# A graph layer and a routed feed-forward layer on one core: the affine branch moved to channels on partitions, and four programs joined into one

## The reference

```python
# layer 1
xh = layernorm(x)
theta = gcn_conv(xh, edges, W1, b1)          # (6250, 64), then only its mean over nodes is used
theta = relu(mean(theta, axis=0)) @ W2 + b2  # (1024,)
theta = 2 * sigmoid(theta) - 1
a0, a1, c0, c1 = per channel, from theta     # a0 = 1 + t0, a1 = t1, c0 = t2 / 2, c1 = t3 / 2
x = x + maximum(xh * a0 + c0, xh * a1 + c1)
# layer 2, 16 experts, 2 chosen for each row
xn = layernorm(x)
logits = xn @ gate_w + gate_b;  top 2, softmax over the two
h = relu(xn @ w1[e] + b1[e]);   y = h @ w2[e] + b2[e]
x = x + layernorm(xn + weighted sum of the two y) * gamma + beta
```

## Time and profile before

| | |
|---|---|
| median of 3 runs | 1049.39 us (1049.09 to 1052.37) |
| the profiled execution's own time | 1059.64 us |
| its span | 1057.8 us |
| mean granted TensorE clock | 0.821 |
| busy: PE / DVE / ACT / POOL | 698.1 / 687.2 / 417.3 / 456.7 us |
| DMA | 178.11 MB, mean 168 GB/s |

### The profile page before, as it was taken

One profiled execution on the slowest core, in us unless ns is written; L12 is line 12 of the kernel. 1 busy time (PEld: TensorE's weight loads), 2 busy tenths in 40 slices (PEclk: granted clock), 3 DMA queues, 4 the chain that ended last, 5 costly groups with the idle time before them and its releaser, 6 DMA issues. The chain is left out here.

```text
span 1057.8 us, 21646 instructions
## 1 busy us (share of the span) xinstructions
PE 698.1 (66%) x6132; PEld 609.6 (58%) x6132; DVE 687.2 (65%) x1486; ACT 417.3 (39%) x1089; POOL 456.7 (43%) x655
## 2 busy tenths in 40 slices
PE   3666878887515334230499999999999999970000
PEld 3553655555204333230399999999999999960000
DVE  7998999999269988812145555555444444435984
ACT  5933777776112222220133333333334333321331
POOL 9200000000002888845057777777555555540422
PEclk9997899999655555555599999999999999995555
DMA  9906756752171342224677766767676676625672
GB/s 290 247 7 49 191 160 159 174 173 52 57 237 51 116 143 98 84 74 141 242 210 216 211 212 212 214 211 212 213 214 211 212 211 213 211 81 174 243 240 70
DMA packets 100597, 178.11 MB, mean 168 GB/s; under 512 B 25247, under 2 KB 69153, under 8 KB 97055
## 3 DMA queue, kind: packets, MB, share of 16 engines
q1 hardware_dynamic: 75092, 145.28, 45.8%
q0 software_dynamic: 10512, 27.88, 7.5%
q10 hardware_dynamic: 14880, 3.60, 2.8%
HBM read 139.53 MB, written 37.20 MB: 167 GB/s over the span
## 5 line engine op out<-in xcount | busy, mean ns | idle before, releaser
L1133 PEld LDWEIGHTS PS<-W 128*128 128x128 f32 x1808 | 221.8, 193 | 8.7 <-issue 2.1
L1133 PE MATMUL PS<-W 128*128 128x128 f32 x1808 | 222.6, 277 | 2.2 <-DMA W<-in_L_ffn_w 1.7
L1144 PE MATMUL PS<-W 128*128 x904 | 213.7, 379 | 0.0
L1144 PEld LDWEIGHTS PS<-W 128*128 128x128 f32 x904 | 164.1, 191 | 17.5
L1291 POOL DMA_INDIRECT ys<-W x113 | 121.6, 1076 | 115.5 <-DVE W L1249 88.2
L691 DVE TENSOR_TENSOR W<-R,W 128x3584 bf16<-128x3584 bf16 (+1 forms) x104 | 159.4, 1590 | 0.0
L859 POOL DMA_INDIRECT xs<-W,slot_i x98 | 120.9, 1234 | 88.2 <-DVE slot_i L1008 59.9
L1221 DVE TENSOR_SCALAR W<-PS,b1T 128x128 f32<-128x128 f32 x226 | 70.2, 347 | 115.3 <-PE PS L1133 84.5
L1174 ACT ACTIVATE W<-PS 128x256 f32<-128x256 f32 x113 | 43.3, 383 | 257.3 <-PE PS L1121 155.2
L544 ACT ACTIVATE W<-PS 112x1024 f16<-112x1024 f32 x104 | 105.7, 1020 | 40.1 <-PE PS L603 38.7
L863 POOL MEMSET R<- 128x261 f32 x1 | 0.3, 317 | 254.3 <-POOLq L360 254.3
(11 more groups left out here) (215 smaller groups left out, 1154.5 us busy)
## 6 DMA issues: line engine op xcount, KB each, us to landing
W<-in_L_ffn_w SPq DMA_DIRECT2D x129, 512.0 KB, 8.8
W<-key_rows SPq DMA_DIRECT2D x26, 896.0 KB
W<-xs SPq DMA_DIRECT2D x113, 130.5 KB
W<-ys SPq DMA_DIRECT2D x6, 1792.0 KB, 8.1
XH<-in_x SPq DMA_DIRECT2D x6, 896.0 KB, 11.2
W<-in_x SPq DMA_DIRECT2D x7, 768.0 KB
out<-W SPq DMA_DIRECT2D x6, 896.0 KB, 4.1
W<-in_L_ffn_b ACTq DMA_DIRECT2D x1, 2048.0 KB, 7.5
```

Of the source, the lines that this page charges most:

```text
L1133: last = nc.tensor.matmul(PS[:, 2 + 2 * u + j // 2, (j % 2) * P:(j % 2 + 1) * P], W1S[:, b, k, j * P:(j + 1) * P], XT3[:, u, k, :], start= ...
L1144: last = nc.tensor.matmul(PS[:, 6 + u, 0:C], HT3[:, u, j, :], wt2(e * W2COLS, j), start=(j == 0), stop=(j == 3))
```

## The change

- The coefficients are columns. W2 and b2 are loaded at the start. Eight small products (instead of two of 512 columns) put the 1024 values of theta on 128 partitions x 8, so that each channel has its four coefficients on its own partition. ScalarE's sigmoid table is loaded ahead (`warm`), and the square root's right after the sigmoid.
- The affine branch works with channels on partitions. A group is cut into a chunk of 4 tiles and one of 3. TensorE turns a chunk of XH into PSUM (`turn1`), ScalarE makes both affine forms of it with scale and bias by partition (`affine`: 4 instructions of 512 or of 384 elements), VectorE takes one maximum (`widest`), TensorE turns the result back (`back`), and VectorE adds x to it straight from PSUM (`add_x`). There is one PSUM area for `turn1`, so chunk q+1 is turned after chunk q has been read.
- `xn` has three buffers (XNBUFS). One PSUM bank holds the turned tiles of `turn2`. The prefix of a group stands in TensorE's order after `turn2` of the next, and VectorE's `route` is split in two, `route` and `place`. Loops are written out.
- x for the first two groups is loaded among the last key loads of the first stage, and the other half of the w2 weights before the rest of x.
- Everything is one `nc.Block()`. SP loads four w1 matrices before it waits for the scattered rows. After the last scatter of the experts SP waits for their landing and loads `ys`.
- In the last stage XH is added by VectorE, not by POOL.

```diff
+                def turn1(q):
+                    g, j0, n = CH[q]
+                    if q >= 1:
+                        pe.wait_ge(affined, q)
+                    for j in range(n):
+                        for k in range(2):
+                            last = nc.tensor.transpose(TA[:, j, k, :], XH[:, DG[g][0] + j0 + j, k * P:(k + 1) * P], ident[:, :])
+                    last.then_inc(turned1, 1)
...
-                act.activation(theta, gb2_bc, ACT.Sigmoid).then_inc(sig_ready, 1)
+                act.activation(zcol[:, :, :], zcol[:, :, :], ACT.Sigmoid).then_inc(sig_ready, 1)
+                act.activation(warm[:, 1:2], ones1[:, :], ACT.Sqrt).then_inc(warmed, 1)
+
+                def affine(q):
+                    g, j0, n = CH[q]
+                    act.wait_ge(turned1, q + 1)
+                    if q >= 2:
+                        act.wait_ge(returned, q - 1)
+                    for k in range(2):
+                        for into, s, c in ((bra, 0, 2), (brb, 1, 3)):
+                            last = act.activation(into[q % 2][:, k, 0:n, :], TA[:, 0:n, k, :], ACT.Identity,
+                                                  bias=coef[:, k, c:c + 1], scale=coef[:, k, s:s + 1])
+                    last.then_inc(affined, 1)
...
+                for i in range(-3, NDG - 1):
+                    for q in GCH[i + 3][1:] if i + 3 < NDG else ():
+                        turn1(q)
+                    if 0 <= i + 4 < NDG:
+                        turn1(GCH[i + 4][0])
+                    if i + 3 < NDG:
+                        back(GCH[i + 3][0])
+                    if 0 <= i + 2 < NDG:
+                        turn2(i + 2)
+                    if 0 <= i + 1:
+                        prefix(i + 1)
+                    for q in GCH[i + 3][1:] if i + 3 < NDG else ():
+                        back(q)
+                    if 0 <= i + 2 < NDG:
+                        gate(i + 2)
...
-                    link(nc.vector.tensor_tensor(branch, rows, cb[0], ALU.mult))
-                    link(nc.vector.tensor_tensor(branch, branch, cb[2], ALU.add))
-                    link(nc.vector.tensor_tensor(rows, rows, cb[1], ALU.mult))
-                    link(nc.vector.tensor_tensor(rows, rows, cb[3], ALU.add))
-                    link(nc.vector.tensor_tensor(rows, rows, branch, ALU.max))
...
+                    nc.vector.tensor_tensor(XH[:, t:t + n, :], TB[:, 0:n, :], x_in[:, g % 2, 0:n, :], ALU.add).then_inc(x_added, 1)
...
+                    nc.vector.tensor_tensor(scaled[u], scaled[u], XH[:, g * GT:(g + 1) * GT, :], ALU.add
+                                            ).then_inc(out_ready, 1)
```

More of the change, by code:

```diff
@@ L40 @@
 NGT = NT // GT
+DG = [(k * GT, GT) for k in range(NGT)]
+NDG = len(DG)
+CH, GCH, T2 = [], [], [0]
+for _g, (_t, _n) in enumerate(DG):
+    GCH.append([])
+    for _j in range(0, _n, 4):
+        GCH[-1].append(len(CH))
+        CH.append((_g, _j, min(4, _n - _j)))
+    T2.append(T2[-1] + -(-_n // 2))
 CAP = 6400
@@ L188, in build @@
         home = take([XBUFS], i32)
+        at[0] = D_AT + 4 * XNBUFS * GT * XW
+        b2_bc = take([E, C], fp32)
         gamma_bc = take([C], fp32)
@@ new lines, in build, with x_loads, sends, pad_row @@
+        tab_ready = sem("tab_ready")
+        tab_turned = sem("tab_turned")
+        tables_out = sem("tables_out")
+        def x_loads(g):
+            return 16 * (g // 2 + 1) + (16 if g == NDG - 1 else 0)
+        def sends(g):
+            return 16 * 2 * sum(DG[h][1] for h in range(g % XNBUFS, g + 1, XNBUFS))
+        def pad_row(eng, e):
+            row = eng.value_load(pad_i[0:1, e:e + 1], min_val=0, max_val=XROWS - P)
+            eng.dma_start(xs[ds(row, P), :], zrows).then_inc(pads_in, 16)
@@ L433, in _ @@
+                prepare(0)
+                for t in range(MT):
+                    if t + 1 < MT:
+                        prepare(t + 1)
+                    if 8 <= t < 8 + NT:
+                        add_beta(t - 8)
+                    send(t)
             @block.sync
@@ new lines, in _, with load @@
+                sp.wait_ge(zrows_set, 3)
+                sp.dma_start(xs[XROWS:XROWS + P, :], zrows).then_inc(pads_in, 16)
+                sp.wait_ge(pads_ready, 1)
+                for e in range(E // 2):
+                    pad_row(sp, e)
+                sp.wait_ge(tables_out, 3)
+                def load(t):
+                    row = sp.value_load(tile_r[0:1, t:t + 1], min_val=0, max_val=XROWS)
+                    sp.dma_start(X3[:, t % XBUFS, :], xs[ds(row, P), :]).then_inc(x3_in[t % XBUFS], 16)
@@ new lines, in gate @@
+                def gate(g):
+                    t, n = DG[g]
+                    pe.wait_ge(turned2_read, T2[g + 1])
+                    if g >= 1:
+                        pe.wait_ge(logits_read, g)
+                        pe.wait_ge(prefix_read, g)
+                    for j in range(n):
+                        for k in range(2):
+                            last = nc.tensor.matmul(PS[:, 7, j * E:(j + 1) * E], xnT[:, j, k, :], gw_sb[:, k, :],
+                                                    start=(k == 0), stop=(k == 1))
+                    last.then_inc(logits_done, 1)
@@ L673, in _ @@
+                down(MT - 1, e_next)
             @block.vector
```

942 lines of the change are left out of this document (461 added, 481 removed).

## The result

The changed kernel takes 1013.05 us, median of 4 runs (1012.48 to 1015.04), the one before 1049.24 beside it: ratio 0.9654, 95% interval 0.9629 to 0.9678. That is 36.2 us faster; 61.0 were forecast, and 1013 lies outside the range of 972 to 1007. The profiled execution has an own time of 1013.3 and a span of 1011.3, where the forecast's steps gave a span of 996.8 (1057.8 less 61.0). Two misses, 24.7 us together, are to be kept apart: 14.5 us between the steps and the trace, and 10.2 us because the steps started from a profile that stood 10.2 us above the median of its runs and were then taken off the median.

What follows compares the result with a forecast made beforehand. POOL and VectorE were taken to bound stage 2 together, VectorE's passes slowing POOL. Gains of 32.7 + 14.0 + 7.3 + 7.0 = 61.0 us, off the median of 1049.39, gave 988.4; range 972 to 1007.

Steps and rivals of the forecast that it cites:

- Before the experts: From stage 2's last scatter to the first expert product: 7.5 us for 21.5, 14.0 gained, bounds 9 and 16.
- landing 2.5: After stage 2's last scatter, ahead of the experts' row load: 2.5 us until the scattered data are there.
- the 32.7: Gain in us up to the end of stage 2's last scatter, forecast at 464.3 where it was 497.04.
- The middle of the two cases: Stage 2's clock: mean of half and full clock, first slots 50 and 40 us, last scatter at 474 and 455.
- the half clock's 50: Start of stage 2, from ScalarE's start to the first slots: 50 us at half clock, 40 at full.
- the ring: Stage 2: TensorE and ScalarE working in fixed order, 20 to 21 us a group at half clock, 15.5 at full.
- The first affine: Start of stage 2: ScalarE starts at 283.6 us, where VectorE started at 287.64.
- POOL's pace: Stage 2: POOL's scatters, held only by the two maxima, take 17.6 + 1.1 = 18.7 us a group.
- The half clock rival: Stage 2 at half clock, and the addition holds POOL too: 474 + 8 = 482, so 1006 us; chance 0.13.
- The gap behind the experts: After the experts' last scatter SP waits 2.2 us for its data; load at 949.3 for 956.65, 7.3 us gained.
- The last stage: Factors no longer stand while POOL adds, and the last addition takes 2.03 us for 3.95: 7.0 us gained.
- The early x loads: Loads placed among block 1's key loads cost nothing; were the keys late, some 5 us.

## Why the prediction was wrong

| step | predicted, us | measured, us | forecast low by |
|---|---|---|---|
| first affine | 283.6 | 287.9 | 4.3 |
| first affine to first scatter | 45 | 49.0 | 4.0 |
| first scatter to the end of the last | 135.7 | 135.0 | -0.7 |
| to the first expert product | 7.5 | 14.3 | 6.8 |
| experts | 428.6 | 428.2 | -0.4 |
| gap behind them | 2.2 | 1.6 | -0.6 |
| last stage | 94.2 | 95.4 | 1.2 |
| sum (span 996.8 and 1011.3) | | | 14.5 |
| profile above its median | 0 | 10.2 | 10.2 |

**The step that failed most**, among those of the sum, is "Before the experts": "After the last scatter: landing 2.5", with the early loads of b2 and w1 priced only where they meet the rows. Measured was a landing of 11.61. Two delays make it, and both have to go: the load of b2 on the same DMA engines (7.1 to 7.4 with b2 held back or issued earlier, with w1 in place or not) and the tile of 106 rows (9.74 with that tile alone sent first, 3.91 and 2.70 with both). The 2.5 was read behind the experts, where neither is there; the earlier trace rows had the warning, the last scatter's 1.56 for 0.96. Nor did the missing border win time by itself here. From the last scatter's end to the row load the kernel before took 11.6 us, 10.0 in its second profile, of which the landing was 5.1 (6.6 from the scatter's start); the changed kernel takes 10.8, all landing but for 0.75. The gain of this stretch lies behind the row load: 3.5 us to the first product for 9.9 and 10.1.

**The base** is the largest single miss, 10.2 us. The prediction noted that its profile stood 1% above the median and then took differences worked out in it off the median. With 10.2 more, the range would have ended at 1017 and the forecast would have been 998.6. The high part was for the most part one stall, the 11.83 in the earlier trace rows, which it used as if every run had it. The second profile of the kernel before has 3.08 there, and scatters 8.6 us shorter. Had I asked which waits a typical run has, the 32.7 would have been about 24.

**The clock.** "The middle of the two cases", 45 us, was a mean of two prices of which one holds: most windows show 0.50 to 0.66, and the first slots took 49.0, the half clock's 50. That the same middle came out for the scatters (135.7, measured 135.0) is luck: at half clock their price was 140. Four groups did take the ring's 20 us, and then POOL took 18.0 for each of the last three, a gain that the prediction named and didn't price. (By its own terms the middle is 464.1, not 464.3.) **The first affine:** 3.9 of its 4.3 us are the later end of `th`, spread between executions. From there it came after 5.9 us (281.94 to 287.87) for the 5.5 forecast, by two errors that nearly cancel: the products took 3.86 instead of 2.5, beyond the bound of 3.5 from the gate's instructions, and the 0.8 for transposes in front of them did not come. The gate's instructions were the wrong measure, since their pace goes with the clock and that of these products doesn't: 3.86 us at a granted clock of 1.00 here (282 to 285), and 3.86 in the run with the short tile first, where the same window shows 0.50.

**What held.** The ring of 20 to 21 us at half clock (its terms add up to 19.6): 20.1, 21.2, 20.3 and 19.5 between groups where it closed, and splitting the gate, its longest link, gave 8 us. POOL's pace, 18.7 forecast: 18.1 once nothing else bounds. The half clock rival ("1006, the addition holds POOL too") had the clock right and the hold wrong; nor do its 8 us follow, since with another 0.8 POOL's 18.7 stays below the ring's 20. The rule cited from the Trainium skill, "SBUF — State Buffer", Who interferes with whom, holds in one half: the addition with one SBUF input beside 0.96 scatters. Its inference that tensor_tensor leaves descriptor writing alone doesn't hold here: 1.79 beside the maximum of 1024 elements. The gap behind the experts: 7.3 forecast, 8.0 measured, and a drain of POOL brings it back. The last stage: 7.0 forecast, 5.8 measured against the kernel before, 6.8 when the addition alone was put back, and the factors at 0.17 as said. The early x loads: no cost in block 1. (That VectorE "is never short" of keys was not quite so: in the kernel before it waited for them once, 2.4 us at L718.)

## What to carry to other kernels

Before a difference is taken off a median, look for what the profiled execution has that the median hasn't, if need be by a second profile: a stall in one place is not the change's to win. When a border between stages goes, the transfers that it kept apart meet: price the last small transfers beside each bulk load that now starts earlier, and put that load where the DMA engines have room. Where two delays end in one wait, taking either away shows little. In a ring of engines, find the longest single link and cut it, and send the odd-sized tile first, not last.

## What the hardware showed that was not expected

- An indirect scatter of 106 rows takes POOL 1.56 us for 0.96 with 128 rows, and as the last one lands 7.1 to 7.4 us after its start, with 0.13 of the DMA engines busy meanwhile, where a last scatter of 128 rows took 2.70, and one of `ys` 2.39.
- With a drain of POOL behind its indirect scatters the next load comes 9.4 us after the last of them, though the data land in 2.4.
- Sixteen small products (64 x 128 weights, one column) take 3.86 us at a granted clock of 1.00 and, but for their first half microsecond, of 0.50 alike.
- A tiny VectorE instruction (128x7, two tensors in) issued beside POOL's addition of 3.95 us takes 3.91 for 0.17.
- The clock differs between executions of the same code: the gate of the second group took 5.99 us in most profiles and 3.27 in that of the run with the short tile first, whose code is the same up to the last group and whose window from 320 to 340 shows 0.76 for 0.50. Its own time of 1003.55 stands 6.8 us below its median. Times of single profiles were therefore compared stage by stage only.
